# A graph layer in float32: the row sums turned into rows by a DRAM scratch, the adjacency loads issued by ScalarE's queue, the first batches in another order

## The chip, the cores and the metric

The kernel runs on one core of one Trainium2 chip. Its time is the device time of one execution in microseconds (us), lower is better. Before the change three runs gave 213.66, 214.75 and 214.75 us, median 214.75. One more execution was profiled; all rows below are from it.

The engines go by short names: PE is TensorE (matmul), PEld its weight load, DVE is VectorE, ACT is ScalarE, POOL is GpSimd, SP is SyncE, which here only issues DMA transfers.

## What is computed

For each of 16 batches there are 512 nodes with 128 features `x` and a 512x512 adjacency matrix `adj`. Layer norm and a ReLU give `h`. Seven relations each give a 512x128 result; the maximum over them, plus a bias and `x`, is the output.

```python
h = jnp.maximum(_layernorm(x, axis=-1), 0.0)
HW  = einsum('bnf,rfo->rbno', h, W[:, :F]) + einsum('rd,rdo->ro', W_edges, W[:, F:])[:, None, None, :]
A   = stack([adj, adj, shifted, adj^T, adj^T, shifted^T, eye])
AHW = einsum('rbnm,rbmo->rbno', A, HW)
out = x + max(AHW, axis=0) + b
```

The second einsum is one constant row c per relation. For the four relations that use `adj` or its transpose, multiplying by A turns this constant into (row sum of A) x c, so the kernel needs the row sums of `adj` and of `adj^T` for each batch.

## The kernel before

Everything is kept with features on the partitions and the 512 nodes along the row. float32 products are made of three products of the faster float32r type: each operand is split into a high part (a rounded copy, made by ACT) and a low part (the rest, a subtraction on DVE or POOL). One batch b goes through these stages on PE:

- gT: `bank_gT` = h times `adj`, 1 whole chunk in float32, then 9 matmuls of split operands (L787 to L799).
- turn_h: four 128x128 transposes of h (L729).
- g: `bank_g` = h times `adj^T`, the same way (L808 to L819).
- turn_sums: four 128x128 matmuls with the identity (L737) turn the row sums, which lie down the partitions, into rows. POOL had spread them into `sum_parts` (L298, L302); ACT copies the result to `sumsT` (L466).
- H products: three relations that use h alone, three matmuls each (L848 to L850).
- sums' products: four matmuls of 32 rows each (L838), one per relation with an adjacency, that start the accumulation in four banks.
- six matmuls on gT (relations 3 and 4), then six on g (relations 0 and 1).

DVE takes the running maximum `best` over the seven products as they come (`take_best(b, i)`, L626 for H, L629 for the rest; L473 on ACT begins it). POOL adds `x_bias` to it (L318, `finish`). `x_bias` is made by a load of the bias on SP's queue (L245) and a load of x that adds into it, issued by POOL (L310, `add_bias`).

Each engine runs its instructions in the order in which the code writes them and waits for semaphores in between. DVE's order in the loop for b is: statistics of x for b+2 (L542, L549), low parts of `adj^T` for b (L592), scale and shift for b+1 (L576, L578), gT_lo, hT_lo, low parts of `adj` for b+1 (L585), h_lo of b+1 (L598), g_lo, then the maxima. The last chunk's low part is made on POOL (L324 for `adj`, after h_lo; L330 for `adj^T`, after `add_bias`). SP's order for b is: x of b+3, `adj` of b+2, store of b-1, bias of b+1, `adj^T` of b+2. Two buffers each hold `adj` and `adj^T`, so a load for b+2 waits until b has been used (`sums_ready`, `gT_psum`, `g_psum`, `alo_ready`).

Of the kernel before, what the change touches and what calls it, by code (L numbers as in the profile page):

```python
# [5 lines left out]
ALU = mybir.AluOpType  # L6
# [21 lines left out]
FIRST = 2  # L28
NX = 4


def gnn_kernel(nc: bass.Bass, x: bass.AP, xT: bass.AP, adj: bass.AP, adjT: bass.AP, W: bass.AP,
               W_rel: bass.AP, W_edges: bass.AP, biasT: bass.AP, outT: bass.AP):
# [11 lines left out]
    w_dram = W[:, :F, :].rearrange("r f o -> f r o")  # L45

    with ExitStack() as ctx:
# [37 lines left out]
        sumsT = sb("sumsT", [P, N], F32R)  # L85
# [7 lines left out]
        std = sb("std", [P, C])  # L93
        rstd = sb("rstd", [P, C])
        shift = sb("shift", [P, C])
# [84 lines left out]
        sumsT_ready = sem("sumsT_ready")  # L180
        hT_psum = sem("hT_psum")
# [31 lines left out]
        def _(sp):  # L213
# [7 lines left out]
            def load_adj(b):  # L221
                q = b % 2
                if b >= 2:
                    sp.wait_ge(sums_ready, 2 * (b - 2) + 1)
                    sp.wait_ge(gT_psum, b - 1)
                if b >= 2 + FIRST:
                    sp.wait_ge(alo_ready, (b - 1 - FIRST) * ND)
                    sp.wait_ge(alo_last_ready, b - 1 - FIRST)
                sp.dma_start(adj_sb[q][:, :, :], adj_dram[b]).then_inc(adj_in[q], 16)

            def load_adjT(b):
                q = b % 2
                if b >= 2:
                    sp.wait_ge(sums_ready, 2 * (b - 2) + 2)
                    sp.wait_ge(g_psum, b - 1)
                if b >= 2 + FIRST:
                    sp.wait_ge(aTlo_ready, (b - 1 - FIRST) * ND)
                    sp.wait_ge(aTlo_last_ready, b - 1 - FIRST)
                sp.dma_start(adjT_sb[q][:, :, :], adjT_dram[b]).then_inc(adjT_in[q], 16)
# [24 lines left out]
            load_adj(1)  # L264
            load_adjT(1)
            load_x(2)
            load_bias(0)
            load_adj(2)
            load_adjT(2)
            load_bias(1)  # L270
            load_x(3)
# [18 lines left out]
        def _(pool):  # L290
            def part_sums(b):
# [3 lines left out]
                if b >= 2:  # L295
                    pool.wait_ge(sumsT_psum, b - 1)
# [644 lines left out]
```

## Time and profile before

| what | value |
|---|---|
| median of 3 runs | 214.75 us (213.66 to 214.75) |
| the profiled execution | 213.96 us |
| its span, first to last instruction | 212.1 us |
| PE busy | 204.4 us (96%) |
| DVE busy | 175.5 us (83%) |
| ACT busy | 160.7 us (76%) |
| POOL busy | 89.4 us (42%) |
| bytes moved | 51.06 MB, 241 GB/s over the span |

The span leaves out 1.86 us of the execution (213.96 less 212.1), which lie before the first and after the last instruction. Shares are averages over the whole span. Batches 3 to 15 repeat one pattern, batches 0 to 2 have waits of their own, and after the last product only DVE and a store are left.

### The profile page before, as it was taken

Reading aid. Unit: us, or ns where it says so; the run is one execution under the profiler, and the core shown is the slowest. Engines: PE = TensorE matmul, PEld = TensorE weight load, DVE = VectorE, ACT = ScalarE, POOL = GpSimd, SP = SyncE. Lnnn points to the kernel's source line nnn. Section 1 sums busy time; section 2 is a strip of 40 time slices with the busy share of each in tenths; the row PEclk is TensorE's granted clock in tenths of the full one; section 3 lists DMA queues with packets and bytes.
Section 4 is the critical chain, followed back from the end, with each engine's and each line's share of the span. In section 5 each row is a group of like instructions: output and inputs, shape, how many; then the busy total and the mean of one; then the engine's idle time right before and its main releaser. Section 6 shows DMA issues by size and latency. Waiting matters only on the chain.

```text
span 212.1 us, 3382 instructions
## 1 busy us (share of the span) xinstructions
PE 204.4 (96%) x894; PEld 147.0 (69%) x894; DVE 175.5 (83%) x411; ACT 160.7 (76%) x432; POOL 89.4 (42%) x138
## 2 busy tenths in 40 slices
PE   7998989999999999999999999999999999999992
PEld 7556457766777677777777777777767777776771
DVE  3487849999799897979889797988989799997755
ACT  4887889696969869696987969697696968785230
POOL 3041232955256615437261633624473272726200
PEclk9999999999999999999999999999999999999999
DMA  5999999897988959497894959689794959833101
GB/s 161 336 364 371 348 343 281 214 311 205 338 223 306 293 132 400 107 378 196 262 331 141 391 104 385 172 266 292 200 388 88 384 122 299 245 99 53 49 2 49
DMA packets 33746, 51.06 MB, mean 241 GB/s; under 512 B 1872, under 2 KB 11328, under 8 KB 33728
## 3 DMA queue, kind: packets, MB, share of 16 engines
q1 hardware_dynamic: 31152, 46.53, 64.1%
q0 software_dynamic: 2304, 4.20, 12.5%
q8 instruction: 7, 0.11, 0.2%
q10 hardware_dynamic: 272, 0.13, 0.2%
q14 instruction: 11, 0.09, 0.1%
HBM read 46.65 MB, written 4.19 MB: 240 GB/s over the span
## 4 chain that ended last, share of the span: by engine, by line
PE 82%; DVE 6%; DMA 6%; issue 2%; SPq 1%; ACT 1%; POOL 0%; DVEq 0%; ACTq 0%; POOLq 0%
PE bank_p L848 11%; PE bank_p L850 9%; PE bank_p L849 9%; DMA x_sb<-in_x_dram 6%; PE bank_g L808 5%; PE bank_gT L787 5%; PE bank_gT L799 4%; PE bank_g L819 4%; PE bank_g L813 4%; PE bank_gT L793 4%; PE bank_g L812 4%; PE bank_gT L792 4%; PE bank_p L729 3%; PE bank_p L838 3%; PE bank_p L737 2%; DVE best L629 2%
## 5 line engine op out<-in xcount | busy, mean ns | idle before, releaser
L324 POOL TENSOR_TENSOR a_lo<-adj_sb,a_hi 128x512 fp32r<-128x512 f32 x14 | 18.2, 1298 | 52.7 <-DVE h_lo L598 50.6
L629 DVE TENSOR_TENSOR best<-bank_p,best 128x512 f32<-128x512 f32 x48 | 33.2, 691 | 7.5 <-PE bank_p L850 6.3
L626 DVE SCALAR_TENSOR_TENSOR best<-bank_p,c_col,best 128x512 f32<-128x512 f32 x32 | 24.0, 750 | 9.3 <-ACT best L473 8.4
L454 ACT ACTIVATE gT_hi<-bank_gT 128x512 fp32r<-128x512 f32 x16 | 9.6, 597 | 29.1 <-PE bank_gT L799 28.2
L310 POOL DMA_DIRECT2D x_bias<-in_xT_dram x16 | 14.0, 876 | 34.5 <-DMA x_bias<-in_biasT_dram 34.5
L436 ACT ACTIVATE h<-x_sb,shift,rstd 128x128 f32<-128x128 f32 x60 | 24.7, 487 | 2.2 <-DVE shift L578 2.2
L407 ACT ACTIVATE a_hi<-adj_sb 128x512 fp32r<-128x512 f32 x42 | 25.9, 622 | 0.2 <-DMA adj_sb<-in_adj_dram 0.2
L420 ACT ACTIVATE aT_hi<-adjT_sb 128x512 fp32r<-128x512 f32 x42 | 25.9, 624 | 0.0
L592 DVE TENSOR_TENSOR aT_lo<-adjT_sb,aT_hi 128x512 fp32r<-128x512 f32 x28 | 23.9, 891 | 0.0
L330 POOL TENSOR_TENSOR aT_lo<-adjT_sb,aT_hi 128x512 fp32r<-128x512 f32 x14 | 22.0, 1569 | 1.2 <-ACT aT_hi L420 1.2
L318 POOL TENSOR_TENSOR o_sb<-best,x_bias 128x512 f32<-128x512 f32 x15 | 20.0, 1332 | 5.9 <-DMA x_bias<-in_xT_dram 3.0
L792 PE MATMUL bank_gT<-a_hi,h_hi 128*128 128x512 f32 x42 | 22.1, 525 | 0.0
L812 PE MATMUL bank_g<-aT_hi,h_hi 128*128 128x512 f32 x42 | 22.1, 525 | 0.0
L848 PE MATMUL bank_p<-hT_hi,w_hi 128*128 128x512 f32 x48 | 20.5, 427 | 0.8 <-ACT sumsT L466 0.7
L850 PE MATMUL bank_p<-hT_lo,w_hi 128*128 128x512 f32 x48 | 19.0, 395 | 0.0
L849 PE MATMUL bank_p<-hT_hi,w_lo 128*128 128x512 f32 x48 | 18.8, 393 | 0.0
L585 DVE TENSOR_TENSOR a_lo<-adj_sb,a_hi 128x512 fp32r<-128x512 f32 x28 | 18.8, 712 | 0.0
L793 PE MATMUL bank_gT<-a_hi,h_lo 128*128 128x512 f32 x42 | 16.5, 393 | 0.0
L813 PE MATMUL bank_g<-aT_hi,h_lo 128*128 128x512 f32 x42 | 16.5, 393 | 0.0
L542 DVE BATCH_NORM_STATS2 stats<-x_sb 128x6 f32<-128x128 f32 x60 | 12.9, 277 | 3.1 <-DMA x_sb<-in_x_dram 3.1
L613 DVE TENSOR_TENSOR g_lo<-bank_g,g_hi 128x512 fp32r<-128x512 f32 x16 | 11.0, 688 | 4.2 <-ACT g_hi L460 4.2
L808 PE MATMUL bank_g<-adjT_sb,h 128*128 128x512 f32 x28 | 14.3, 594 | 0.0
(126 smaller groups left out, 517.4 us busy)
## 6 DMA issues: line engine op xcount, KB each, us to landing
adj_sb<-in_adj_dram SPq DMA_DIRECT2D x15, 1024.0 KB, 5.7
adjT_sb<-in_adjT_dram SPq DMA_DIRECT2D x15, 1024.0 KB, 7.7
x_bias<-in_biasT_dram SPq DMA_DIRECT2D x16, 256.0 KB, 5.9
x_bias<-in_xT_dram POOLq DMA_DIRECT2D x16, 256.0 KB, 4.7
x_sb<-in_x_dram SPq DMA_DIRECT2D x15, 256.0 KB, 8.0
out_dram<-o_sb SPq DMA_DIRECT2D x15, 256.0 KB, 5.8
adj_sb<-in_adj_dram SPq DMA_DIRECT2D x4, 256.0 KB, 5.3
adjT_sb<-in_adjT_dram SPq DMA_DIRECT2D x4, 256.0 KB, 5.2
```

The lines of the kernel that those rows point to most:

```text
L407: nc.scalar.activation(a_hi[q][:, i, :], adj_sb[q][:, c, :], ACT.Copy, accum_out=sums[q][:, 0, c:c + 1]).then_inc(ahi_ready, 1)
L420: nc.scalar.activation(aT_hi[q][:, i, :], adjT_sb[q][:, c, :], ACT.Copy, accum_out=sums[q][:, 1, c:c + 1]).then_inc(aThi_ready, 1)
L436: last = nc.scalar.activation(h[q][:, c, :], x_sb[b % NX][:, c, :], ACT.Relu, bias=shift[:, c:c + 1], scale=rstd[:, c:c + 1])
L629: op = nc.vector.tensor_tensor(best[q][:, :], product, best[q][:, :], ALU.max)
L792: nc.tensor.matmul(bank_gT[:, 0:N], h_hi[q][:, i, :], a_hi[q][:, i, :], start=False, stop=False)
L793: nc.tensor.matmul(bank_gT[:, 0:N], h_lo[q][:, i, :], a_hi[q][:, i, :], start=False, stop=False)
L808: nc.tensor.matmul(bank_g[:, 0:N], h[q][:, c, :], adjT_sb[q][:, c, :], start=(c == WHOLE[0]), stop=False)
L812: nc.tensor.matmul(bank_g[:, 0:N], h_hi[q][:, i, :], aT_hi[q][:, i, :], start=False, stop=False)
L813: nc.tensor.matmul(bank_g[:, 0:N], h_lo[q][:, i, :], aT_hi[q][:, i, :], start=False, stop=False)
L848: nc.tensor.matmul(dst, w_hi[:, i, :], hi[:, nodes], start=start, stop=False)
L849: nc.tensor.matmul(dst, w_lo[:, i, :], hi[:, nodes], start=False, stop=False)
L850: return nc.tensor.matmul(dst, w_hi[:, i, :], lo[:, nodes], start=False, stop=stop)
```

## The change

Five things change, together.

1. From batch 2 on (`TURNED`) the row sums are turned another way. DVE makes high and low parts of the 8 sums per partition (two instructions of 128x16) and transposes the 128x32 tile in blocks (`turn_blocks`). SP writes that tile, 16 KB, to a scratch in DRAM, waits for it, and reads it back by four transfers of 4x16 pieces of 32 elements into four rows of each group of `sumsT`, which now has two buffers (`turn_sums`). The matmuls of L737, ACT's copy L466 and POOL's L298 and L302 are gone for these batches.
2. On PE the sums' products stand behind the products on gT, no longer ahead of them. The products of relations 3 and 4 are then complete only when the sums' products have run.
3. From batch 3 on `adj` and `adj^T` are loaded by ACT (`load_adj` behind the split of hT, `load_adjT` behind `begin_best`).
4. std, rstd and shift have two buffers, and are made one batch ahead.
5. In the first batches: batch 0 runs the product of relation 1 ahead of the last H product, whose bank waits for `sumsT`; batch 1 makes h_lo and g_lo ahead of the statistics of batch 3; x of batch 3 is loaded ahead of `adj` of batch 2.

```diff
+            def turn_sums(b):            # SP
+                i = b - TURNED + 1
+                q = b % 2
+                sp.wait_ge(blocks_turned, i)
+                sp.dma_start(scratch, sum_blocks[:, :]).then_inc(scratch_in, 16)
+                sp.wait_ge(scratch_in, 16 * i)
+                sp.wait_ge(prod_psum, (b - 1) * NPROD)
+                for g in range(len(ORDER_A)):
+                    sp.dma_start(sumsT[q][g * GROUP:g * GROUP + 4, :].rearrange("r (c j s) -> r c j s", c=C, s=GROUP)
+                                 .bitcast(F32), scratch_rows[g // 2]).then_inc(sumsT_in[q], 16)
             for b in range(1, B):
+                if b >= TURNED:
+                    turn_sums(b)
                 if b + 3 < B:
                     load_x(b + 3)
-                if b + 2 < B:
-                    load_adj(b + 2)
                 store(b - 1)
                 if b + 1 < B:
                     load_bias(b + 1)
-                if b + 2 < B:
-                    load_adjT(b + 2)
...
+            def turn_blocks(b):          # DVE
+                q = b % 2
+                i = b - TURNED + 1
+                s = sums[q][:, :, :].unsqueeze(2).to_broadcast([P, 2, 2, C])
+                dve.wait_ge(sums_ready, 2 * b + 2)
+                nc.vector.tensor_copy(sum_cols[:, :, :, 0, :], s).then_inc(cols_hi, 1)
+                dve.wait_ge(cols_hi, i)
+                nc.vector.tensor_tensor(sum_cols[:, :, :, 1, :], s, sum_cols[:, :, :, 0, :].bitcast(F32),
+                                        ALU.subtract).then_inc(cols_lo, 1)
+                dve.wait_ge(cols_lo, i)
+                if i >= 2:
+                    dve.wait_ge(scratch_in, 16 * (i - 1))
+                nc.vector.transpose(sum_blocks[:, :], sum_cols[:, :, :, :, :].rearrange("p d k s c -> p (d k s c)")
+                                    .bitcast(F32)).then_inc(blocks_turned, 1)
...
-                turn_sums(b)             # PE
+                if b < TURNED:
+                    turn_sums(b)
                 for i in range(NH):
                     product(b, i)
-                begin_products(b)
-                for i in range(NH, NPROD - int(b == B - 1)):
+                pe.wait_ge(gTlo_ready, b + 1)
+                for i in range(NH, NH + len(AT_RELS)):
+                    passes(i, bank_of[i][:, 0:N], start=True)
+                take_sums(b)
+                for i in range(NH + len(AT_RELS), NPROD - int(b == B - 1)):
                     product(b, i)
```

PE, batch 2 before the change, from the last of g to the first product on g (`sumsT` are the rows of sums, `bank_g` the bank of the last relation):

```order
L819 MATMUL bank_g<-aT_lo,h_hi 128x512 x3
L737 MATMUL bank_p<-ident_r,sum_parts 128x128 x4
L848 MATMUL bank_p<-hT_hi,w_hi 128x512
...
L850 MATMUL bank_p<-hT_lo,w_hi 128x512
L838 MATMUL bank_p<-sumsT,c_rows 128x512 x3
L838 MATMUL bank_g<-sumsT,c_rows 128x512
L848 MATMUL bank_p<-gT_hi,w_hi 128x512
```

PE, the same place after:

```order
L870 MATMUL bank_g<-aT_lo,h_hi 128x512 x3
L905 MATMUL bank_p<-hT_hi,w_hi 128x512
...
L907 MATMUL bank_p<-gT_lo,w_hi 128x512
L895 MATMUL bank_p<-sumsT,c_rows 128x512 x3
L895 MATMUL bank_g<-sumsT,c_rows 128x512
L905 MATMUL bank_p<-g_hi,w_hi 128x512
```

Four matmuls are gone from each batch, and the four of the sums moved down behind six on gT.

DVE, from g_lo of a batch to the statistics in the next, before (`stats` belong to b+2, `best` to b):

```order
L613 TENSOR_TENSOR g_lo<-bank_g,g_hi 128x512
L626 SCALAR_TENSOR_TENSOR best<-bank_p,c_col,best 128x512 x2
L629 TENSOR_TENSOR best<-bank_p,best 128x512 x3
L629 TENSOR_TENSOR best<-bank_g,best 128x512
L542 BN_STATS stats<-x_sb 128x6 x4
```

and after:

```order
L643 TENSOR_TENSOR g_lo<-bank_g,g_hi 128x512
L671 SCALAR_TENSOR_TENSOR best<-bank_p,c_col,best 128x512 x2
L674 TENSOR_TENSOR best<-bank_p,best 128x512 x3
L651 CAST sum_cols<-sums 128x4x4
L653 TENSOR_TENSOR sum_cols<-sums,sum_cols 128x4x4
L658 STREAM_TRANSPOSE sum_blocks<-sum_cols 128x32
L674 TENSOR_TENSOR best<-bank_g,best 128x512
L569 BN_STATS stats<-x_sb 128x6 x4
```

Three instructions on the sums of b+1 now stand ahead of the last maximum of b.

SP's queue over one batch, before:

```order
L219 DMA x_sb<-in_x_dram 128x4x128
L229 DMA adj_sb<-in_adj_dram 128x4x512
L249 DMA out_dram<-o_sb 128x512
L245 DMA x_bias<-in_biasT_dram 128x512
L239 DMA adjT_sb<-in_adjT_dram 128x4x512
```

and after:

```order
L236 DMA scratch_dram<-sum_blocks 128x32
L241 DMA sumsT<-scratch_dram 4x16x32 x4
L229 DMA x_sb<-in_x_dram 128x4x128
L252 DMA out_dram<-o_sb 128x512
L248 DMA x_bias<-in_biasT_dram 128x512
```

The two large loads have left for ACT's queue, and the load of x, the store and the bias stand behind the scratch write, its landing and four reads.

## Rows read from the trace of the kernel before

**Rows 1.** The page's part 1: busy time, share of the span, instructions.

```profile
PE 204.4 (96%) x894; PEld 147.0 (69%) x894; DVE 175.5 (83%) x411; ACT 160.7 (76%) x432; POOL 89.4 (42%) x138
```

**Rows 2.** The chain that ended last, in time order: start us, length us, piece.

```profile
48.16 0.86 PE bank_gT L787 x2
...
97.30 0.86 PE bank_gT L787 x2
...
103.61 0.40 PE bank_p L737 x4
104.00 0.28 PE bank_p L848
...
106.15 0.42 PE bank_p L838 x2
...
109.59 0.86 PE bank_gT L787 x2
...
195.62 0.86 PE bank_gT L787 x2
...
205.92 0.70 DVE best L629
```

**Rows 3.** Timeline, DVE in one batch: start, us, operation, [idle before <-releaser].

```profile
98.10 0.86 DVE L542 BATCH_NORM_STATS2 stats<-x_sb 128x6 f32<-128x128 f32 x4
...
101.61 0.68 DVE L603 TENSOR_TENSOR hT_lo<-bank_p,hT_hi 128x512 fp32r<-128x512 f32 x1
...
104.28 0.69 DVE L613 TENSOR_TENSOR g_lo<-bank_g,g_hi 128x512 fp32r<-128x512 f32 x1 [0.23 <-ACT g_hi L460]
105.56 1.54 DVE L626 SCALAR_TENSOR_TENSOR best<-bank_p,c_col,best 128x512 f32<-128x512 f32 x2 [0.59 <-ACT best L473]
107.60 2.14 DVE L629 TENSOR_TENSOR best<-bank_p,best 128x512 f32<-128x512 f32 x3 [0.51 <-PE bank_p L850]
```

**Rows 4.** Timeline, waits in the first batches.

```profile
29.49 0.87 DVE L542 BATCH_NORM_STATS2 stats<-x_sb 128x6 f32<-128x128 f32 x4 [3.06 <-DMA x_sb<-in_x_dram]
31.97 0.50 PE L838 MATMUL bank_p<-sumsT,c_rows 32*128 32x512 f32 x3 [1.08 <-DVE g_lo L613]
43.77 0.19 PEld L848 LDWEIGHTS bank_p<-hT_hi,w_hi 128*128 128x128 f32 x1 [0.57 <-ACT sumsT L466]
```

**Rows 5.** Timeline, a DMA that ACT issues, ACT's wait and copy, a small DVE instruction.

```profile
0.80 0.48 ACTq L476 DMA_DIRECT2D x_sb<-in_x_dram  x1
...
100.27 0.60 ACT L454 ACTIVATE gT_hi<-bank_gT 128x512 fp32r<-128x512 f32 x1 [1.99 <-PE bank_gT L799]
100.93 0.16 DVE L578 SCALAR_TENSOR_TENSOR shift<-mean_var,rstd 128x4 f32<-128x4 f32 x1
...
104.14 0.59 ACT L466 ACTIVATE sumsT<-bank_p 128x512 fp32r<-128x512 f32 x1
```

**Rows 6.** DMA issues by tensor: transfers, KB each, median us from issue to landing.

```profile
x_bias<-in_biasT_dram SPq DMA_DIRECT2D x16, 256.0 KB, 5.9
...
out_dram<-o_sb SPq DMA_DIRECT2D x2, 128.0 KB, 1.7
```

**Rows 7.** Timeline, SP's issues of one batch and what POOL does with the bias.

```profile
100.31 0.37 SPq L229 DMA_DIRECT2D adj_sb<-in_adj_dram  x1
...
101.27 0.43 SPq L245 DMA_DIRECT2D x_bias<-in_biasT_dram  x1
...
107.44 0.86 POOL L310 DMA_DIRECT2D x_bias<-in_xT_dram  x1 [2.02 <-DMA x_bias<-in_biasT_dram]
108.05 1.59 POOL L330 TENSOR_TENSOR aT_lo<-adjT_sb,aT_hi 128x512 fp32r<-128x512 f32 x1
```

**Rows 8.** Timeline, the one batch in which the bias came late.

```profile
145.94 0.88 POOL L310 DMA_DIRECT2D x_bias<-in_xT_dram  x1 [3.66 <-DMA x_bias<-in_biasT_dram]
...
149.81 1.28 POOL L318 TENSOR_TENSOR o_sb<-best,x_bias 128x512 f32<-128x512 f32 x1
149.87 1.23 DVE L578 SCALAR_TENSOR_TENSOR shift<-mean_var,rstd 128x4 f32<-128x4 f32 x1
```

More of the change, by code:

```diff
@@ L92, in gnn_kernel @@
         mean_var = pair("mean_var", [P, C, 2])
-        std = sb("std", [P, C])
-        rstd = sb("rstd", [P, C])
-        shift = sb("shift", [P, C])
+        std = pair("std", [P, C])
+        rstd = pair("rstd", [P, C])
+        shift = pair("shift", [P, C])
         eps = sb("eps", [P, 1])
@@ L180, in gnn_kernel @@
         sumsT_ready = sem("sumsT_ready")
+        cols_hi = sem("cols_hi")
+        cols_lo = sem("cols_lo")
+        blocks_turned = sem("blocks_turned")
+        scratch_in = sem("scratch_in")
+        sumsT_in = [sem(f"sumsT_in{i}") for i in range(2)]
         hT_psum = sem("hT_psum")
@@ L404, in split_adj @@
                     act.wait_ge(gT_psum, b - 1)
[L405 removed]
+                if b < 2 + TURNED:
+                    act.wait_ge(parts_lo, b - 1)
+                else:
+                    act.wait_ge(cols_lo, b - 1 - TURNED)
                 for i, c in enumerate(SPLIT):
@@ L436, in make_h @@
                     last = nc.scalar.activation(h[q][:, c, :], x_sb[b % NX][:, c, :], ACT.Relu,
-                                                bias=shift[:, c:c + 1], scale=rstd[:, c:c + 1])
+                                                bias=shift[q][:, c:c + 1], scale=rstd[q][:, c:c + 1])
                 last.then_inc(h_ready, 1)
@@ L481, in _ @@
             act.wait_ge(half_aggr_done, 1)
-            nc.scalar.activation(std[:, 0:HALF], mean_var[0][:, 0:HALF, 1], ACT.Sqrt,
+            nc.scalar.activation(std[0][:, 0:HALF], mean_var[0][:, 0:HALF, 1], ACT.Sqrt,
                                  bias=eps[:, :]).then_inc(half_std_ready, 1)
@@ L485, in _ @@
             for c in range(HALF):
-                nc.scalar.activation(h[0][:, c, :], x_sb[0][:, c, :], ACT.Relu, bias=shift[:, c:c + 1],
-                                     scale=rstd[:, c:c + 1]).then_inc(half_h_ready, 1)
+                nc.scalar.activation(h[0][:, c, :], x_sb[0][:, c, :], ACT.Relu, bias=shift[0][:, c:c + 1],
+                                     scale=rstd[0][:, c:c + 1]).then_inc(half_h_ready, 1)
             act.wait_ge(aggr_done, 1)
-            nc.scalar.activation(std[:, HALF:], mean_var[0][:, HALF:, 1], ACT.Sqrt,
+            nc.scalar.activation(std[0][:, HALF:], mean_var[0][:, HALF:, 1], ACT.Sqrt,
                                  bias=eps[:, :]).then_inc(std_ready, 1)
@@ L492, in _ @@
             for c in range(HALF, C - 1):
-                last = nc.scalar.activation(h[0][:, c, :], x_sb[0][:, c, :], ACT.Relu, bias=shift[:, c:c + 1],
-                                            scale=rstd[:, c:c + 1])
+                last = nc.scalar.activation(h[0][:, c, :], x_sb[0][:, c, :], ACT.Relu, bias=shift[0][:, c:c + 1],
+                                            scale=rstd[0][:, c:c + 1])
             last.then_inc(h_ready, 1)
@@ L691, in _ @@
             split_adj_lo(2)
-            for i in range(NH, NPROD):
+            scale_and_shift(3)
+            for i in range(NH, NPROD - 1):
                 take_best(1, i)
+            turn_blocks(2)
+            take_best(1, NPROD - 1)
             for b in range(2, B):
@@ L706, in _ @@
                 split_g_lo(b)
-                for i in range(1, NPROD - int(b == B - 1)):
+                for i in range(1, NPROD - 1):
                     take_best(b, i)
+                if b + 1 < B:
+                    turn_blocks(b + 1)
+                    take_best(b, NPROD - 1)
             b, q = B - 1, (B - 1) % 2
@@ L874, in products_first @@
                 turn_sums(0)
-                product(0, 2)
                 pe.wait_ge(crow_ready, 1)
```

133 lines of the change are left out of this document (73 added, 60 removed).

## The prediction

> **What bounds the kernel now.** I read the page's part 1 first: PE is busy 96% of the span, DVE 83% [rows 1]. Then the chain of waits. From batch 3 to batch 15 it is PE alone, the same pieces in each batch: gT begins at 48.16 in batch 3 and at 195.62 in batch 15, so (195.62 - 48.16) / 12 = 12.29 us per batch [rows 2]. Every microsecond taken from PE's work there counts twelve times, as long as nothing else becomes late. So next I read DVE's timeline over one batch [rows 3]. The reader is to see that it pauses only three times, 0.23 + 0.59 + 0.51 = 1.33 us. DVE thus works 12.29 - 1.33 = 10.96 us per batch. That is the second bound, and it is near. ACT waits 1.99 us once a batch [rows 5]. The first batches are another stage: PE stands there for DVE and ACT [rows 4].
>
> Below, times within a batch count from the start of gT (97.30 in the batch shown).
>
> **PE in a repeated batch.** The four turning matmuls take 0.40 us, and the first product behind them 0.28 where its neighbours take about 0.24 [rows 2]. Removed: 0.40 to 0.44, taken as 0.42. The four 32-row matmuls only move. They still run together in 0.42, and there is still one change into this form and one out of it. So PE alone would make a batch in 12.29 - 0.42 = 11.87 us.
>
> **DVE in a repeated batch.** Three instructions come in. None of them is in the trace. The nearest row is the small `shift` with 0.16 us [rows 5], plus about 0.04 for the hand-over from one to the next, as each waits for the one before: 3 x 0.20 = 0.6 us. Bounds: 0 (all three in the waits that DVE has anyway) and 2.0 (three of hT_lo's 0.68, a 512-wide one [rows 3]). I take 0.6, since the tiles are 16 and 32 wide. DVE then works 11.56 us of 11.87, with 0.31 left.
>
> Does the new place hurt? g ends at 6.31 (103.61), H products at 8.46, six products on gT at about 9.9, the sums' products at 10.33. The third maximum starts at about 10.43. Three maxima take 2.14, the turn 0.6, the last maximum 0.7: 13.9, which is 2.0 in the next batch, where it was 0.80 before (98.10). DVE runs 1.2 us later against PE. `hT_lo` ended at 4.99 (101.61 + 0.68). Now it ends at 4.99 + 1.2 less 0.3 for the scale and shift that moved behind it, 5.9, and PE asks for it at 6.31. Slack 0.4. The last maximum frees the bank of g at 2.0, asked for at 3.4. So PE remains the bound, narrowly.
>
> **ACT.** It loses the copy, 0.59, and gains two issues of 0.48 [rows 5]: 0.37 more, within its 1.99 of waiting. Its std now depends on DVE's later statistics, so about 1 us of that wait is used as well. Cost taken 0. Without the cover it would be 0.4 per batch. `adj` of b+2 is issued some 1 us later and is used about 6 us after that, about what a loaded transfer takes to land (5.9 [rows 6]); a later one would first use up what is left of ACT's wait.
>
> **SP and the scratch.** The tile is turned at 13.9 - 0.7 - 11.87 = 1.3. The write lands 1.7 us later if it is like the last stores, 5.9 if like the bias [rows 6]. Four issues of 0.43 follow, the last one starting 1.3 after the first [rows 7], and its landing takes again 1.7 to 5.9. The rows are there between 1.3 + 1.7 + 1.3 + 1.7 = 6.0 and 14.4, and PE asks at 9.9. For the write I take 2.0, as only the end of the `adj^T` load is in flight then; for the read 3.5, since `adj` starts beside it. That gives 8.1, in time by 1.8. The cost is 0, and at the upper end 4.5 us per batch.
>
> The page "DMA: Bandwidth & Descriptors" of the Trainium skill, "Anatomy of one DMA", gives a transfer about 2.0 us that do not depend on its size, mostly the receipt of the last byte, and warns that it can be surprisingly long when the target is HBM. By that rule two small transfers in a row cost 4.0 us plus the issues, and the rows come at 6.6. The trace's 1.7 for a store to DRAM agrees [rows 6].
>
> **POOL** loses about 1 us of work per batch and is no bound by its load.
>
> **The first batches.** PE's waits of 1.08 for g_lo (DVE was held 3.06 us for x of batch 3) and 0.57 for `sumsT` go [rows 4]. The product of relation 1 fills about 0.3 in batch 0. The turning matmuls of batch 2 go, 0.42. Together 2.37. But DVE is without a pause in this stretch and now has the statistics and the turn ahead of the last maximum of batch 1, for which g of batch 2 waits. I put what is given back at 1.1 (bounds 0 and 2.4). Net 1.25: gT of batch 3 at 46.9 instead of 48.16.
>
> **The end.** After the last product DVE is the chain, from the third maximum on. It started 10.30 after gT (205.92 - 195.62) and now starts at 10.43: 0.1 lost.
>
> **Sum**, against the profiled execution's 213.96 (span 212.1 and 1.86 around it): 213.96 - 1.25 - 12 x 0.42 + 0.1 = 207.8. With 0.3 us of slack DVE can't absorb what it absorbed before. In one of twelve batches the bias landed late, and `shift` took 1.23 us beside POOL's addition [rows 8]. I allow for two such batches at 0.8 each: 209.4. The profiled run is 0.8 under the median and within the runs' spread, so I leave the number as it is.
>
> **Rival 1: DVE's turn collides with POOL, and the kernel is slower.** In rows 8 `shift`, which reads two SBUF operands, begins 0.06 after POOL's o_sb and ends with it: 1.23 us for work of 0.16. The last `adj^T` part on POOL takes 1.59 and starts 0.61 after the bias has landed [rows 7]. Before, DVE then took maxima out of PSUM, at normal length. Now the turn stands there. Count from the end of one turn. The scratch write takes 2.0, the reads 1.75, x and the store 1.0, so the bias is issued at 4.75. If it lands after l, POOL's part runs from 5.36 + l to 6.95 + l, and the turn begins at about 11.3. From l = 4.35 DVE waits, its next turn ends at about 7.45 + l, and this repeats itself. At l = 4.85 a batch is as long as before. At l = 5.2 it is 12.65 us, and the time 213.96 - 1.25 + 12 x 0.36 + 0.1 = 217.1. For it: the bias took 5.9 before. Against it: it then followed 1.25 MB in one queue, now 0.5 MB; with l over about 6 POOL's part falls behind the turn; and a longer batch leaves the transfers freer. The place is the three turn instructions, and what decides is where POOL's L330 lies.
>
> "GPSIMD Engine Reference" of the Trainium skill, section "Key points", says that GpSimd shares its SBUF interfaces with VectorE, with contention for VectorE instructions with two SBUF inputs or in a two-port mode. The 1.23 us of rows 8 agree; by it the subtraction, and perhaps the copy, of the turn are such instructions.
>
> **Rival 2: collisions in about half of the batches.** The phase moves after each stall, so the batches alternate. A batch of 12.1 on average gives 213.96 - 1.25 - 12 x 0.19 + 0.1 = 210.5.
>
> **Rival 3: the rows of sums come late.** The turn waits for the maxima, these for the sums' products, and these for the scratch: a loop. Its other parts are 0.1 + 2.14 + 0.6 + 1.3 + 0.42 = 4.6, so it holds back PE when the two landings exceed 11.87 - 4.6 = 7.3 us together. At 8.3 a batch takes 12.87 and the time is about 219.8. For it: 5.9 under load. Against it: 1.7 when free, and 16 KB.
>
> **Rival 4: DVE is full.** If the turn takes 1.3, a batch is 12.26, and only the first batches gain: about 212.5.
>
> **How the numbers follow.** The forecast case, 207 to 210.5 around 209.4, has 0.42. Rival 2 (209.5 to 212) 0.16. Rival 1 (212 to 221) 0.25. Rival 3 (213 to 222) 0.08. Rival 4 0.09. What a measurement here tells from no change is about 0.5%, 1.1 us. Faster: 0.42 + 0.15 and a part of rival 4, 0.60. Within 0.5%: 0.11, from rivals 1 and 4. Slower: 0.29. The range from 206.6 to 217.5 leaves out the lower tail of the forecast and the upper half of rivals 1 and 3. The forecast's own range is 207 to 210.5.
>
> **What the profile after would show.** PE 5.6 us less busy, by the 56 turning matmuls. The distance from gT to gT 11.9 (12.3 or more for the rivals). The three turn instructions near 0.16 each; near 1.3 for one of them would be rival 1, with POOL's L330 (now L333) beside it. No wait of PE's sums' products on the load of `sumsT` (rival 3). Batch 3's gT near 46.9. I am wrong if DVE shows no pause and PE waits for hT_lo or for the last maximum in every batch.

## The result and the profile after

The kernel after takes 228.95 us (median of 4 runs, 227.36 to 230.46), the kernel before 214.22 (4 runs, 213.66 to 214.75). The ratio is 1.068, 95% interval 1.062 to 1.074: slower, by 14.7 us. The prediction was 209.4, with 0.29 for slower. The sign is wrong, and the time lies above the range (206.6 to 217.5). The profiled execution took 230.46, its span 228.6. One run each of `e_pe_turn` (217.4), `v_best_early` (222.3) and `e_adj_behind` (249.71) below was a slow one; the medians count them, the ratios do not.

In short: two things ate the gain. The rows of sums arrived after PE asked for them. And the bias, now behind the scratch on SP's queue, came so late that POOL's instructions ran beside DVE's and stretched them.

The page's part 1 of the kernel after [rows 1], and what it lists of waits (releaser: us in total, times, longest):

```profile
PE 205.9 (90%) x838; PEld 142.1 (62%) x838; DVE 193.4 (85%) x453; ACT 153.4 (67%) x418; POOL 76.1 (33%) x82
```

```profile
POOL x_bias L313 <- DMA x_bias<-in_biasT_dram: 56.3, 15, 6.6
...
PEld bank_p L895 <- DMA sumsT<-scratch_dram: 11.2, 8, 2.9
...
PE bank_p L895 <- DMA sumsT<-scratch_dram: 7.9, 7, 2.5
...
PEld bank_g L870 <- DVE aT_lo L622: 7.1, 11, 2.5
```

PE runs 56 matmuls less, as forecast, but is busy 1.5 us more (part of it at a lower clock, see below) and no longer the bound. The chain of waits, which was PE alone from batch 3 on [rows 2], now has four main parts, and the load of `sumsT` leads its lines:

```profile
PE 39%; DVE 24%; DMA 22%; issue 7%; SPq 6%; ACT 0%; POOL 0%; DVEq 0%; POOLq 0%
DMA sumsT<-scratch_dram 16%; DVE best L674 11%; DMA scratch_dram<-sum_blocks 6%; SPq L241 6%; PE bank_p L905 6%; PE bank_p L907 5%; PE bank_p L906 5%; DVE aT_lo L622 4%; PE bank_p L895 3%; DVE sum_cols L651 3%; PE bank_g L870 2%; PE bank_gT L802 2%; DVE stats L569 2%; PE bank_p L941 2%; PE bank_g L828 2%
```

gT begins at 51.55 in batch 3 and at 212.01 in batch 15: 13.37 us per batch, where it was 12.29 and 11.87 was forecast. The batches are not alike, they take 11.7 to 15.6 us. Batch 2 takes 17.6 (33.91 to 51.55), before it took 12.7. All starts of gT here are the timeline's, which puts them 0.17 us ahead of the chain's in [rows 2]. The kernel before, batches 2 and 3:

```profile
35.31 1.02 PE L787 MATMUL bank_gT<-adj_sb,h 128*128 128x512 f32 x2
...
47.99 1.02 PE L787 MATMUL bank_gT<-adj_sb,h 128*128 128x512 f32 x2
```

**The loop.** One batch of the timeline, from the sums' products to the next ones (a wait in brackets, with its releaser; x2 is two instructions in a row):

```profile
101.99 0.50 PE L895 MATMUL bank_p<-sumsT,c_rows 32*128 32x512 f32 x3 [0.68 <-DMA sumsT<-scratch_dram]
102.59 2.14 DVE L674 TENSOR_TENSOR best<-bank_p,best 128x512 f32<-128x512 f32 x3 [1.05 <-PE bank_p L895]
103.92 1.02 PE L838 MATMUL bank_gT<-adj_sb,h 128*128 128x512 f32 x2
104.65 0.16 DVE L651 CAST sum_cols<-sums 128x16 fp32r<-128x16 f32 x1
104.85 0.18 DVE L653 TENSOR_TENSOR sum_cols<-sums,sum_cols 128x16 fp32r<-128x16 f32 x1
105.06 0.21 DVE L658 STREAM_TRANSPOSE sum_blocks<-sum_cols 128x32 f32<-128x32 f32 x1
105.30 0.33 SPq L236 DMA_DIRECT2D scratch_dram<-sum_blocks  x1
107.43 2.62 SPq L241 DMA_DIRECT2D sumsT<-scratch_dram  x4
107.64 0.38 ACTq L486 DMA_DIRECT2D adj_sb<-in_adj_dram  x1
111.58 0.43 SPq L248 DMA_DIRECT2D x_bias<-in_biasT_dram  x1
116.28 0.58 PE L895 MATMUL bank_p<-sumsT,c_rows 32*128 32x512 f32 x3 [2.48 <-DMA sumsT<-scratch_dram]
119.54 1.24 PE L838 MATMUL bank_gT<-adj_sb,h 128*128 128x512 f32 x2
```

Read the gaps. Sums' products to maxima 0.60; three maxima to the turn 2.06; turn 0.65; write issued to landed 2.13; four reads issued 2.62; end of the last issue to the rows' arrival 6.23. Together 14.29. That is the loop of rival 3 (rows, sums' products, maxima, turn, write, reads, rows again), and it is longer than PE's 11.87.

**The collision.** In batch 4, three batches earlier, the bias is late, and the first instruction of the turn lasts as long as POOL's subtraction beside it, 1.66 us instead of 0.16:

```profile
63.92 0.86 POOL L313 DMA_DIRECT2D x_bias<-in_xT_dram  x1 [3.30 <-DMA x_bias<-in_biasT_dram]
64.48 1.66 DVE L651 CAST sum_cols<-sums 128x16 fp32r<-128x16 f32 x1
64.52 1.58 POOL L333 TENSOR_TENSOR aT_lo<-adjT_sb,aT_hi 128x512 fp32r<-128x512 f32 x1
...
70.29 0.68 DVE L633 TENSOR_TENSOR hT_lo<-bank_p,hT_hi 128x512 fp32r<-128x512 f32 x1
...
71.06 0.47 PE L905 MATMUL bank_p<-hT_hi,w_hi 128*128 128x512 f32 x1 [0.51 <-issue]
```

The delay goes on down DVE's queue to `hT_lo`, which ends at 70.97, 7.2 us after gT. PE starts its first product on h 0.09 later, at 7.3, where in batch 14, without a delay, it starts at 6.3. The profile names no releaser for this stand ("issue"), but PE's code waits there for `hT_lo`. The same stand, 0.4 to 0.5 us of idle time, is in 8 of the batches.

In batch 2 both of POOL's instructions come back to back behind the late bias, and DVE's low part of `adj^T` stands through both, 3.49 us instead of 0.7. PE waits 2.03 for it:

```profile
38.57 0.86 POOL L313 DMA_DIRECT2D x_bias<-in_xT_dram  x1 [5.25 <-DMA x_bias<-in_biasT_dram]
39.04 3.49 DVE L622 TENSOR_TENSOR aT_lo<-adjT_sb,aT_hi 128x512 fp32r<-128x512 f32 x1
39.17 1.58 POOL L333 TENSOR_TENSOR aT_lo<-adjT_sb,aT_hi 128x512 fp32r<-128x512 f32 x1
40.42 1.55 POOL L321 TENSOR_TENSOR o_sb<-best,x_bias 128x512 f32<-128x512 f32 x1
42.58 1.33 PE L870 MATMUL bank_g<-aT_lo,h_hi 128*128 128x512 f32 x3 [2.03 <-DVE aT_lo L622]
```

**The clock.** Each row gives a stretch, its length, the busy time of PE, PEld, DVE, ACT and POOL, then three more numbers, the first of which is TensorE's granted clock as a share of 2.4 GHz:

```profile
110.24:113.80 3.56, 3.56 (x16) 2.63 (x14) 3.56 (x6) 3.47 (x10) 1.78 (x2) 1.00 1.01 294
116.28:119.54 3.26, 3.26 (x11) 2.34 (x12) 2.32 (x5) 0.47 (x2) 0.00 (x0) 0.54 0.97 374
44.40:48.00 3.60, 3.57 (x9) 2.83 (x10) 3.20 (x7) 2.45 (x7) 1.28 (x1) 0.57 1.02 300
```

After the stand of 2.48 us PE runs the sums' products and those on g almost at the level of 1.2 GHz: 3.26 us for what takes 1.93 after the stand of 0.68 (101.99 to 103.92). So this wait cost 2.48 + 1.33 us. The same follows the stand of 2.03 in batch 2 (44.40 to 48.00, granted clock 0.57). After the other stands for the rows, 1.24 us and less, the stretch took 1.92 to 1.94.

### The profile page after: what moved, and what is told of

Same layout as the page of the kernel before. It is cut to its first block, busy times and chain, and to the rows that moved or that the text cites. A ratio compares the mean times of both kernels' runs of the same rounds, so it can differ in the third digit from the quotient of the medians.

```text
span 228.6 us, 3294 instructions
## 1 busy us (share of the span) xinstructions
PE 205.9 (90%) x838; PEld 142.1 (62%) x838; DVE 193.4 (85%) x453; ACT 153.4 (67%) x418; POOL 76.1 (33%) x82
## 4 chain that ended last, share of the span: by engine, by line
PE 39%; DVE 24%; DMA 22%; issue 7%; SPq 6%; ACT 0%; POOL 0%; DVEq 0%; POOLq 0%
DMA sumsT<-scratch_dram 16%; DVE best L674 11%; DMA scratch_dram<-sum_blocks 6%; SPq L241 6%; PE bank_p L905 6%; PE bank_p L907 5%; PE bank_p L906 5%; DVE aT_lo L622 4%; PE bank_p L895 3%; DVE sum_cols L651 3%; PE bank_g L870 2%; PE bank_gT L802 2%; DVE stats L569 2%; PE bank_p L941 2%; PE bank_g L828 2%
## 5 line engine op out<-in xcount | busy, mean ns | idle before, releaser
L622 DVE TENSOR_TENSOR aT_lo<-adjT_sb,aT_hi 128x512 fp32r<-128x512 f32 x28 | 33.1, 1222 | 0.0
L313 POOL DMA_DIRECT2D x_bias<-in_xT_dram x16 | 14.0, 875 | 56.3 <-DMA x_bias<-in_biasT_dram 56.3
L382 ACT ACTIVATE std<-mean_var,eps 128x4 f32<-128x4 f32 x15 | 4.4, 296 | 39.7 <-DVE mean_var L576 39.7
L321 POOL TENSOR_TENSOR o_sb<-best,x_bias 128x512 f32<-128x512 f32 x15 | 21.4, 1429 | 14.0 <-DVE best L674 11.3
L907 PE MATMUL bank_p<-hT_lo,w_hi 128*128 128x512 f32 x48 | 19.6, 407 | 0.0
L906 PE MATMUL bank_p<-hT_hi,w_lo 128*128 128x512 f32 x48 | 19.4, 403 | 0.0
L870 PE MATMUL bank_g<-aT_lo,h_hi 128*128 128x512 f32 x42 | 13.6, 417 | 3.6 <-DVE aT_lo L622 3.2
L905 PEld LDWEIGHTS bank_p<-hT_hi,w_hi 128*128 128x128 f32 x48 | 9.3, 194 | 9.8 <-issue 7.8
```

Source lines behind the costliest of these rows:

```text
L622: nc.vector.tensor_tensor(aT_lo[q][:, i, :], adjT_sb[q][:, c, :], aT_hi[q][:, i, :].bitcast(F32), ALU.subtract).then_inc(aTlo_ready, 1)
L905: nc.tensor.matmul(dst, w_hi[:, i, :], hi[:, nodes], start=start, stop=False)
L906: nc.tensor.matmul(dst, w_lo[:, i, :], hi[:, nodes], start=False, stop=False)
L907: return nc.tensor.matmul(dst, w_hi[:, i, :], lo[:, nodes], start=False, stop=stop)
```

## The experiments

Two theories stood at the start. **Late rows**: PE waits for the reads, and that is the loss. **Late bias**: the scratch holds up the bias on SP's queue, and POOL's instructions then lie beside DVE's. The medians below stand against the kernel before in the same series (214.47 to 214.65). Intervals are 95% ones of the ratio.

### No transfers at all, and transfers that nobody waits for

`e_no_rows` leaves the write and the reads out, `e_spare` reads into a tile that nothing uses. In both the sums' products use the rows of batches 0 and 1 for all later batches. In `e_spare`, and in every kernel below with an earlier turn, SP's write also waits until the reads of the batch before have landed, since PE's wait no longer sees to that.

```diff
 # e_no_rows
-                if b >= TURNED:
-                    turn_sums(b)             # SP
 # e_spare
-                    sp.dma_start(sumsT[q][g * GROUP:g * GROUP + 4, :] ...
+                    sp.dma_start(spare[q][g * GROUP:g * GROUP + 4, :] ...
 # both
-                    pe.wait_ge(sumsT_in[b % 2], 64 * (b // 2))
```

> Leaves out the scratch write and its four reads; from batch 2 on the sums' products use the sums of batches 0 and 1. DVE's three turn instructions stay. SP's queue is free for x, the store and the bias. If the scratch transfers are the cause, by their landing or by what stands behind them on SP's queue, a batch falls from 13.4 to about 11.9 to 12.1 us and the time to about 209 to 211. If collisions of POOL with DVE come from the new order itself, it stays above 216. If the adjacency loads on ACT's queue are the cause, it stays near 225.

> The scratch write and the four reads run as in the changed kernel, but the reads land in a tile that nothing uses, and the sums' products of batches 2 to 15 use the sums of batches 0 and 1: PE never waits for the rows. SP's queue is held as before. If the wait for the rows is the whole cause, this is as fast as the kernel without the transfers (about 210). If the late bias behind them (POOL's part of adj^T beside DVE) counts as well, it stays between, 216 to 224, with low parts of adj^T of 1.5 us and more on DVE in most batches.

Measured: `e_no_rows` 210.10 (ratio 0.978, 0.976 to 0.980), `e_spare` 223.86 (1.042, 1.040 to 1.044). Of the way from 210.10 to 228.95, 13.8 us come with transfers alone and 5.1 with the waits for them, in this order of adding them. The waits of the two, first `e_no_rows`, then `e_spare`:

```profile
POOL x_bias L311 <- DMA x_bias<-in_biasT_dram: 16.0, 12, 5.8
```

```profile
POOL x_bias L320 <- DMA x_bias<-in_biasT_dram: 52.1, 16, 7.0
PEld bank_g L877 <- DVE aT_lo L629: 9.0, 9, 3.4
...
PE bank_g L877 <- DVE aT_lo L629: 6.0, 3, 3.1
```

With the scratch on SP's queue POOL waits for the bias 52.1 us instead of 16.0, DVE's instructions are stretched (an `aT_lo` of 3.6, a turn copy of 1.74), and PE waits for DVE: for `aT_lo` (the rows above) and for `hT_lo` (3.6 us in 8 stands, under "issue"). PE never stands for `adj` or its transpose from batch 2 on. So the transfers, through the late bias and without any late row, make the kernel slower than before. Nearly half of it lies in one batch of 18.1 us, with a stand of 3.06 for `aT_lo` and 6.8 us at the lower clock behind it. In `e_no_rows` batches 3 to 14 take 141.04 / 12 = 11.75 us each, at full clock, but batch 2 still takes 17.2.

### The old turn with everything else of the change

```diff
-                if b < TURNED:
-                    turn_sums(b)             # PE
+                turn_sums(b)
```

(and with it L298, L302 and L466 for all batches, without the scratch and `turn_blocks`)

> The row sums turned on PE again (four matmuls, ACT's copy, POOL's parts), with all else of the change: sums' products behind those of gT, adjacency loads from ACT's queue, two buffers of std, first batches reordered. If the scratch is the cause of the loss: 210 to 214, as PE's 12.29 us a batch come back and the first batches keep a gain of 1 to 2 us. If the loads on ACT's queue or the new order cost time: above 218.

Measured: 214.85 (1.000, 0.997 to 1.004), 12.18 us a batch, but batch 2 takes 18.4. So what else changed (ACT's loads, the products' order, statistics ahead, the first batches) neither costs nor gains in sum. It gains 0.1 us in each repeated batch (12.18 against 12.29) and it does bring a long batch 2. The profiled run took 216.68, 1.8 over the median, so batch 2 was shorter in most runs.

### The bias out of SP's queue, or POOL's order turned

`v_bias_act` lets ACT issue the bias ahead of `adj`; `v_pool` puts POOL's last part of `adj^T` ahead of its wait for the bias.

```diff
 # v_bias_act
-                store(b - 1)                 # SP
-                if b + 1 < B:
-                    load_bias(b + 1)
+                store(b - 1)
...
+                if 2 <= b < B - 1:           # ACT, behind split_hT(b)
+                    load_bias(b + 1)
 # v_pool
-                    add_bias(b + 1)
                     split_adjT_last(b + 1)
+                    add_bias(b + 1)
```

> The changed kernel with the bias load issued by ACT ahead of the adjacency load, no longer by SP behind the scratch reads. If collisions from the late bias are half of the loss, the time falls by 5 to 8 us to 221 to 224, and DVE's low parts of adj^T return to 0.65 to 0.85 us each. If only the rows' landing counts, it stays at 227 to 230.

> The changed kernel with two POOL instructions in the other order: the low part of adj^T ahead of the addition into the bias, so that it no longer waits for the bias load. Every transfer stays. If the collision of that part with DVE is a cause by itself, low parts of adj^T on DVE fall from up to 3.5 us to under 1.8 and the kernel gains 3 to 8 us (221 to 226). If the landing of the rows then takes over as the bound, as it did with the bias on ACT's queue, it gains less than 3 us although the collisions go.

Measured: 228.53 (1.064, 1.060 to 1.068) and 227.10 (1.059, 1.052 to 1.065). Waits in the first:

```profile
PEld bank_p L902 <- DMA sumsT<-scratch_dram: 21.5, 10, 5.4
PE bank_p L902 <- DMA sumsT<-scratch_dram: 17.3, 10, 4.9
...
POOL x_bias L311 <- DMA x_bias<-in_biasT_dram: 4.7, 1, 4.7
```

The collisions are gone (no turn copy over 0.63, no `aT_lo` over 1.78), and nothing is won: PE's wait for the rows grew from 7.9 to 17.3. Half of that is two stands, of 4.9 and 3.9 us, each with 6.8 us at the lower clock behind it: those two batches take 18.3 and 17.2 us, the other ten repeated ones 12.6 on average. The two losses hide each other. A batch that one of them stretches gives the other its time: in the kernel after, batches 5, 8, 10 and 12, with an `aT_lo` of 2.5 to 3.5 us, have no wait for the rows.

### The loop made shorter

`v_turn_early` puts the turn ahead of the third maximum. `v_contig` writes the scratch in the rows' order, so that a read is 4 pieces of 2 KB instead of 64 of 128 B (the reads' own lines are left out below).

```diff
 # v_turn_early
-                for i in range(1, NPROD - 1):
+                for i in range(1, NH):
                     take_best(b, i)
                 if b + 1 < B:
                     turn_blocks(b + 1)
-                    take_best(b, NPROD - 1)
+                for i in range(NH, NPROD - int(b == B - 1)):
+                    take_best(b, i)
 # v_contig
-                sp.dma_start(scratch, sum_blocks[:, :]).then_inc(scratch_in, 16)
+                sp.dma_start(scratch_write, sum_blocks[:, :]).then_inc(scratch_in, 16)
```

> The changed kernel with DVE's turn of the sums of b+1 ahead of the third maximum of b, no longer behind the fifth, so that it does not wait for products that wait for the rows of b. If the loop (rows, sums' products, maxima, turn, write, reads) is what sets 13.4 us a batch, the wait of the sums' products on the rows nearly goes and the time falls to 215 to 221. If the transfers only load SP's queue and the DMA engines, it stays above 224.

> The changed kernel with the scratch laid out in row order: the write stays 128 pieces of 128 B, each of the four reads is 4 rows of 2 KB in place of 64 pieces of 128 B. If the many small pieces make the reads slow, their issue falls from 0.61 to about 0.43 us each, the rows land 1 to 3 us earlier, and the time falls by 3 to 9 us. If only the fixed landing of two transfers in a row counts, it gains under 2 us.

Measured: 220.64 (1.028, 1.025 to 1.032) and 225.76 (1.052, 1.049 to 1.056). In `v_contig` the four issues take 1.3 us instead of 2.6, and PE's idle time for the rows falls from 7.9 to 1.0. Yet only 3.2 us are won, since the collisions stay, and become regular:

```profile
77.14 2.09 DVE L652 CAST sum_cols<-sums 128x16 fp32r<-128x16 f32 x1
77.61 1.58 POOL L334 TENSOR_TENSOR aT_lo<-adjT_sb,aT_hi 128x512 fp32r<-128x512 f32 x1
```

In 10 of its batches the turn's copy takes 1.07 to 2.09 us, DVE is busy 146.8 us from gT of batch 3 to gT of batch 15 (129.4 in `e_no_rows_late` below), and PE stands for `hT_lo` 12 times. That is rival 1 as it was written down. Its sum, 7.45 + l, gives 13.3 us a batch with the bias's median landing here, 5.8; 12.93 was measured, with hardly anything late but the bias. The early turn gives 8.3, the most of any single edit on the scratch. It shortens the loop (PE's wait for the rows falls from 7.9 to 4.4) and it also takes the turn out of POOL's way (no copy over 0.75), so its gain is not the loop's alone.

### POOL's addition of the bias later, and the parts together

"Late" below means: POOL's load of x into `x_bias` for b stands behind finish(b-1), where nothing hurries.

```diff
                     finish(b - 1)            # POOL
+                    add_bias(b)
...
-                    add_bias(b + 1)
                     split_adjT_last(b + 1)
```

`v_contig_late` is `v_contig` with it; `v_best_early` has the early turn besides; `v_best_mid` has the turn ahead of the fourth maximum.

> The changed kernel with the scratch in row order and POOL's late addition, but the turn left behind the fifth maximum. If two causes (slow reads, collisions) make the whole loss, this is at 209 to 213. If the loop through the maxima is needed to explain it, 214 to 220.

> The changed kernel with three repairs together: the turn ahead of the third maximum, the scratch in row order (reads of 2 KB pieces), and POOL's addition of x into the bias of batch b issued behind finish(b-1), so that POOL waits for no bias load. If late rows and collisions of POOL with DVE are all that the change lost, a batch falls to 11.75 to 11.9 us and the time to 208 to 211, faster than before. If the extra small transfers cost something beyond these two, it stays at 213 or more.

> As the one before, but with the turn ahead of the fourth maximum. DVE waited 0.5 us a batch for ACT's sums in the early place; here it should wait less. If DVE's time is what is left, 0.5 to 2 us faster than the early place. If the rows' landing is, it is slower by as much.

Measured: 217.46 (1.015, 1.009 to 1.020), 219.68 (1.024, 1.018 to 1.031) and 217.22 (1.013, 1.006 to 1.019). The late addition alone is worth 225.76 - 217.46 = 8.3 us. Batch 2 then takes 14.2 and the others 12.58. What is left is the wait for the rows, and one of ACT for `adj`, behind which PE never stood:

```profile
PEld bank_p L896 <- DMA sumsT<-scratch_dram: 15.2, 12, 2.3
ACT a_hi L413 <- DMA adj_sb<-in_adj_dram: 13.3, 10, 2.3
...
PE bank_p L896 <- DMA sumsT<-scratch_dram: 10.1, 11, 1.9
```

The early turn, worth 8.3 by itself, adds nothing to this; the expectation of 208 to 211 for it missed, and its other branch (213 or more) came true.

### The ceiling

`e_no_rows_late` is `e_no_rows` with the late addition.

> As the kernel of e_no_rows (no write to the scratch and no reads; the rows of sums are those of batches 0 and 1, in every batch), and POOL's load of x into x_bias for b stands behind finish(b-1), no longer ahead of the last part of adj^T. If the long batch 2 is POOL waiting for the late bias and then doing two additions back to back beside DVE's low parts, batch 2 shrinks from 17.2 to about 14 us, the repeated batches stay at 11.75, and the time falls from 210.1 to about 207, near what the prediction's sum gave without its allowance (207.8). Rival: batch 2 is long because the loads of adj and adj^T of batch 2 come late; then it stays near 17 and the time at 210.

Measured: 206.31 (0.961, 0.959 to 0.963). Batch 2 takes 13.66, and gT of batch 3 begins at 47.55. From there to gT of batch 15:

```profile
47.55:188.19 140.64, 140.64 (x613) 103.02 (x612) 129.39 (x326) 114.19 (x311) 56.33 (x48) 1.00 0.85 257
```

PE is never idle, a batch takes 11.72, and DVE works 129.39 / 12 = 10.78 of it, the turn included. So this is what the change is worth without its transfers: 8.2 us. With contiguous transfers it loses 217.46 - 206.31 = 11.2 again, and PE's idle time for the rows there is 10.1.

### Why the reads land late, and whether PE can ask later

`e_adj_behind` is the kernel after with the load of `adj` behind `begin_best`. `v_behind_late` and `v_behind_mid` are `v_contig_late` and `v_best_mid` with the first product on g ahead of the sums' products, so that PE asks for the rows 0.7 us later.

```diff
 # e_adj_behind, ACT
-                if b + 2 < B:
-                    load_adj(b + 2)
                 ...
                 begin_best(b)
                 if b + 2 < B:
+                    load_adj(b + 2)
                     load_adjT(b + 2)
 # v_behind_*, PE
+                if b < B - 1:
+                    pe.wait_ge(glo_ready, b + 1)
+                    passes(NH + len(AT_RELS), bank_of[NH + len(AT_RELS)][:, 0:N], start=True)
                 take_sums(b)
```

> As after, but ACT issues the load of adj directly ahead of that of adj^T, behind begin_best, some 3 us later. If the reads of the rows land 4.5 to 6.8 us after their issue because 1 MB of adj is in flight beside them, they now land in about 3 us, PE's wait for sumsT (19.1 us idle in all in after) falls under 6, and the bias lands earlier (median wait of POOL for it under 3 a batch). The kernel may still lose elsewhere, since adj comes 3 us later: 220 to 228. Rival: the pieces of the reads themselves (4x16 of 128 B each) are slow; then landing and wait stay as in after, and the time is 229 or above.

> As v_contig_late, and PE runs the first product on g ahead of the sums' products (not in the last batch), so that it asks for the rows 0.7 us later. PE stood 10.1 us for them there, 11 times. If the rows are what is left of the loss, the wait falls to about 3 us and the time from 217.5 to about 211. Rival: DVE, whose last maxima now come 0.7 later too, holds the bank of g or hT_lo, or the loop of turn, write and reads moves along with them; then PE's wait for the rows stays near 10 us or turns into waits for DVE, and the time stays at 216 to 218.

> The same step on v_best_mid, where the turn stands ahead of the second last but two maxima, so that the turn does not wait for the later products. 217.22 there, with PE 8.8 us in wait for the rows. If the rows are the only cause, 210 to 212, faster than before. Rival: DVE is full at 11.56 us of work a batch and the time stays at 215 to 217.

Measured: 244.53 (2 runs, 239.35 and 249.71, too far apart for an interval), 216.94 (1.011, 1.006 to 1.017) and 215.80 (1.006, 1.003 to 1.009). A batch of `e_adj_behind`:

```profile
138.86 0.33 SPq L236 DMA_DIRECT2D scratch_dram<-sum_blocks  x1
143.03 2.60 SPq L241 DMA_DIRECT2D sumsT<-scratch_dram  x4
145.26 0.38 ACTq L486 DMA_DIRECT2D adj_sb<-in_adj_dram  x1
...
147.75 0.50 PE L894 MATMUL bank_p<-sumsT,c_rows 32*128 32x512 f32 x3
```

Here `adj` is issued only at the end of the reads. The rows are there 2.1 us or less after the last issue, and PE does not wait. By the updates of the rows' semaphore in the trace, the landing came 1.5 to 3.0 us after the last issue in 13 of the 14 batches, and 5.2 in one. In the kernel after, with `adj` issued beside the reads, the seven batches in which PE waited show 4.0 to 6.2 us. Its last two batches, which have no `adj` left to load, show 1.5 by the same updates. But the write, which now meets what was put off before, takes 4.2 us to land instead of 2.1 (medians 4.3 and 1.9). So the landing was late where megabytes were in flight beside it, and moving them only moved who was late. The expectation was right on the reads and wrong on the time. PE now stands for `aT_lo`, 7.3 us behind DVE and 5.1 behind POOL, since the bias is later still; ACT waits for `adj` as well, but no stand of PE is put down to that:

```profile
POOL x_bias L313 <- DMA x_bias<-in_biasT_dram: 78.6, 14, 10.1
...
ACT a_hi L412 <- DMA adj_sb<-in_adj_dram: 34.5, 13, 4.6
```

In `v_behind_late` the other branch of the expectation came true, that the loop moves along with PE's later ask:

```profile
122.37 0.50 PE L897 MATMUL bank_p<-sumsT,c_rows 32*128 32x512 f32 x3 [1.12 <-DMA sumsT<-scratch_dram]
...
122.97 2.15 DVE L675 TENSOR_TENSOR best<-bank_p,best 128x512 f32<-128x512 f32 x3 [2.16 <-PE bank_p L897]
...
125.03 0.17 DVE L652 CAST sum_cols<-sums 128x16 fp32r<-128x16 f32 x1
...
127.62 1.32 SPq L242 DMA_DIRECT2D sumsT<-scratch_dram  x4
...
134.41 0.50 PE L897 MATMUL bank_p<-sumsT,c_rows 32*128 32x512 f32 x3
```

The loop takes up to 12.04 us here (122.37 to 134.41, where PE did not wait), and 12.3 to 13.5 from one arrival to the next where PE did wait; PE's own work is 11.72. In the mid form only one maximum stands between rows and turn, and the write goes out about 1.9 us after the sums' products instead of 3.3. But it then lands in 2.0 to 4.4 us instead of 1.9 to 3.4. Its 12.4 us a batch ((196.10 - 47.47) / 12) are the best of all forms with the scratch, and it is still slower than the kernel before. The time is the one that the rival of the expectation named, but not for its reason, a full DVE: DVE pauses for 0.95 us or more in each of these batches.

### The kernel before with the first batches, and the best kernels

`b_head_pool` and `b_head_late` are the kernel before with part 5 of the change (but for the product of relation 1) and with POOL's two orders. `e_pe_turn_late` is `e_pe_turn` with the late addition.

```diff
-            variance(3)
             split_h_lo(2)
             split_g_lo(1)
+            variance(3)
...
             load_bias(0)
+            load_x(3)
             load_adj(2)
```

> The kernel before, with three moves alone: h_lo and g_lo of batch 1 ahead of the statistics of batch 3, x of batch 3 loaded ahead of adj of batch 2, and POOL's low part of adj^T ahead of the addition into the bias. PE's wait of 1.08 us (1.47 with its weight loads) goes. If nothing else becomes late: 212.5 to 213.5, ratio 0.990 to 0.996. If DVE gives it back in batch 2: no change.

> The kernel before with the moves in the first batches and POOL's late addition (POOL waits for no bias load). gT of batch 3 should begin at 46.9 to 47.5 instead of 48.16, and the time be 212.8 to 213.8 against 214.2 (ratio 0.993 to 0.999). If DVE keeps giving the gain back, no change.

> The old turn of the sums on PE, everything else of the change, and POOL's load of x into x_bias for b behind finish(b-1). e_pe_turn gave 214.85 with batch 2 of 18.4 us and 12.18 us for a repeated batch. With batch 2 at about 14 the time is about 211, faster than both kernels. Rival: the four branches of the first batches cost elsewhere what they gain, as in b_head_late, whose first batches ended only 0.3 us earlier; then it is 213 to 214.5.

Measured: 214.27 (0.998, 0.996 to 1.001), 213.63 (0.997, 0.995 to 0.999) and 213.24 (0.993, 0.991 to 0.996). The last two beat the kernel after, and the kernel before by 0.3 and 0.7%; which of them is the faster was not measured side by side. In `b_head_late` gT of batch 3 begins at 47.82, only 0.17 earlier than before, where 46.9 to 47.5 (against 48.16) was expected: batch 2 gives back 0.9 of the 1.1 won. In `e_pe_turn_late` batch 2 shrinks from 18.4 to 13.6 us, as expected; one batch of 12.8 among those of 12.19 takes a part back, and the time is 2 us over what was expected.

## Why the prediction was wrong

In sums, from medians of several series: 214.56 before; -8.2 for the change without its transfers and without collisions (`e_no_rows_late`); +3.8 for POOL's order around the bias (`e_no_rows`, nearly all of it in batch 2); +13.8 for transfers in the queues (`e_spare`); +5.1 for the waits on them: 228.95. The last two depend on the order in which they are added, as `v_bias_act` shows. The prediction had the first term and, of the others, 1.6 us for a late bias and nothing for the rows.

- **PE in a repeated batch, right in kind, too small.** 0.42 was taken; gT to gT shrank by 12.29 - 11.72 = 0.57 (0.54 in `e_no_rows`). The turning rows showed 0.40 to 0.44. Another 0.1 belongs to the new order and not to the removal, since `e_pe_turn`, which keeps the four matmuls, also has it (12.18).
- **DVE in a repeated batch, right.** The three instructions take 0.62 us in the rows above (104.65 to 105.27), forecast 0.6. DVE is not full: in `e_no_rows_late` it pauses 0.66 us in each repeated batch, and rival 4 falls. There `hT_lo` ends 5.7 us after gT, forecast 5.9. But the slack of 0.4 was all that stood between a stretched instruction and PE, and 8 stands in the kernel after are for `hT_lo`.
- **SP and the scratch, the first step that failed: cost 0.** Chosen: write 2.0, issues 1.3, read 3.5, rows at 8.1 after gT, cost 0. Measured in the batch shown: write 2.13, issues 2.62, then 6.23 more; rows 12.4 after gT (12.2 by the chain's start). Two terms were mis-sized. An issue of 64 small pieces costs 0.61 us, not the 0.43 of a plain load. And the read lands like a loaded transfer (5.9 in [rows 6]), not between. In the kernel after PE stood 7.9 us for the rows, and the waits cost 5.1 beyond the transfers. The bounds of 6.0 to 14.4 held the truth; what was wrong was the value taken between ends far apart, although the largest load, of 1 MB, starts at the very moment of the reads. Rival 3 stated the right mechanism and the right condition (the landings against 7.3 us) and got 0.08. Its condition is met even in the batch of `v_behind_late` shown, in which PE did not wait: 1.94 + 5.5 = 7.4.
- **The bias, the second step that failed, and the larger one.** The sum allowed two late landings at 0.8 us, since one of twelve had been late before. Measured: POOL waited for it 15 times, 56.3 us in all (34.5 before), and with nobody waiting for the rows the transfers alone cost 13.8 us (`e_spare`). Rival 1 had the mechanism right, and it came together with rival 3. The text treated the two as alternatives. They share one cause, the scratch ahead of everything on SP's queue, and feed each other: `v_bias_act` and `v_pool` remove one and keep the time. The rival also looked at the turn alone. The larger stretch was at `aT_lo` (up to 3.5 us), with both POOL instructions back to back. "GPSIMD Engine Reference" of the Trainium skill, section "Key points", names contention with GpSimd on the shared SBUF interfaces; these rows agree and give its size, the whole of POOL's 1.6 us, or of two such.
- **The first batches, wrong by sign.** Gained until gT of batch 2: 35.31 - 33.91 = 1.40 (forecast 2.37, with 0.42 of it in batch 2). Given back in batch 2: 17.64 - (12.68 - 0.42) = 5.4 instead of 1.1. The rows show the stand of 2.03 for `aT_lo` and the lower clock after it. With the late addition and no transfers 1.4 is won and 1.4 given back by the same count, and gT of batch 3 comes at 47.55, a net gain of 0.44 (the turning matmuls' share) where 1.25 was forecast.
- **The end, right**: 228.6 - 212.01 = 16.6, before 212.1 - 195.45 = 16.65.
- **The clock was no term at all.** As long as PE never stood it was none. The wait of 2.48 us cost 1.33 more.

"DMA: Bandwidth & Descriptors" of the Trainium skill, "Anatomy of one DMA", gives about 2.0 us as the fixed cost of a transfer; its section is on transfers that GpSimd issues, while these are SP's. The writes of this kernel (median 1.9) and the read shown of `e_adj_behind` (2.1 at most) agree; the reads beside a load of `adj` (4.0 to 6.2) do not, and there the measurement decides. The page's warning of a surprisingly long delay names writes to HBM above all, and in the kernel after the write, at 1.4 to 2.4 us, was not the one that was late: the reads were.

## What to carry to other kernels

Price a small transfer that something waits for by what is in flight at the moment of its issue, and write down the loop it closes: when work, write, read and landing together come near the length of a batch, the transfer is the bound, and a later ask does not help. A new entry at the head of a queue delays all behind it, so look for the instruction that comes late with the last of them, and for what runs beside it. When two rivals share a cause, give them a chance together.

## What the runs showed of the hardware

- Issue time went with the pieces: on SP 0.61 us for a read of 64 pieces of 128 B, 0.30 for one of 4 pieces of 2 KB, of the same 8 KB (medians of 56). In `v_contig` the write's issue grew from 0.33 to 0.52.
- The reads landed 1.5 us after the last issue in the two batches of the kernel after that have no load of `adj` beside them, and 3.9 to 6.2 in the twelve beside 1 MB of `adj`. Contiguous reads under the same load took 3.4 to 5.2 in `v_contig` and 5.2 to 6.2 in `v_contig_late`. So size and pieces mattered less than company.
- A DVE copy of 128x16 out of SBUF with 0.16 us of work took 1.66 beside a POOL subtraction of 1.58. In `v_contig` it took 2.09: it began 0.47 ahead of the subtraction, beside POOL's DMA issue of 0.87. Maxima out of PSUM were not stretched, none took over 0.76 in any run.
- Stands of PE of 2.03 and 2.48 us were followed by stretches at a granted clock of 0.57 and 0.54, those of 1.24 and less in that kernel by none. A stand of 1.9 was followed by the lower level in `v_best_early` and not in `v_contig_late` and `v_best_mid`.
